# First attention of a two-layer kernel: attention sums in float32r parts over normed tokens, low parts on GpSimd, value weights applied to the sums

## The reference, cut to what matters

```
h = layernorm(x) * (1 + ca) + sa             # per batch; x1 = layernorm(x) before scale and shift
Q = (h @ Wq.T)  K = (h @ Wk.T)  V = (h @ Wv.T)   # per head
attn = softmax(Q @ K.T)                      # 1024 x 1024 per batch and head
out = sum over heads of attn @ V
x = x + ga * out
```

## Time and profile before

| | |
|---|---|
| median of three runs | 3593.37 us (3593.08 to 3593.81) |
| the profiled execution | 3593.08 us, its span 3591.3 us |
| first scores of the attention | 81.67 us into the span |
| last attention output added to x | about 2005 us |
| PE busy | 3069.3 us (85%) |
| DVE busy | 2606.2 us (73%) |
| ACT busy | 1313.8 us (37%) |
| POOL busy | 184.3 us (5%) |

### The profile page before, as it was taken

The page is one execution under the profiler, slowest core; times in us unless marked ns, Lnnn a source line. Parts: engine busy times, 40 slices in busy tenths (PEclk is TensorE's granted clock), DMA queues, the critical chain, the costliest instruction groups (busy, mean ns, idle before and its releaser), DMA issues. The chain is left out here.

```text
span 3591.3 us, 82463 instructions
## 1 busy us (share of the span) xinstructions
PE 3069.3 (85%) x32284; PEld 2455.2 (68%) x32284; DVE 2606.2 (73%) x8488; ACT 1313.8 (37%) x2231; POOL 184.3 (5%) x155
## 2 busy tenths in 40 slices
PE   5999999999999999999999568778888887763555
PEld 2888888888888888888888535555656555551222
DVE  4565766756657667566565579999999999946775
ACT  2544454454545545445454122222222222211222
POOL 0000000000000000000000000000000000002220
PEclk9999999999999999999999856766666666666777
DMA  1000000000000000000000110000000000000000
GB/s 64 1 1 7 1 1 7 1 2 7 1 7 1 1 8 1 1 7 1 7 1 1 45 48 0 0 0 0 0 0 0 0 0 0 0 10 7 12 12 18
DMA packets 6415, 25.26 MB, mean 7 GB/s; under 512 B 1360, under 2 KB 1872, under 8 KB 5840
## 3 DMA queue, kind: packets, MB, share of 16 engines
q1 hardware_dynamic: 6224, 22.57, 1.6%
HBM read 14.18 MB, written 8.39 MB: 6 GB/s over the span
## 5 line engine op out<-in xcount | busy, mean ns | idle before, releaser
L605 PEld LDWEIGHTS obank<-v_one,probs 128*128 128x128 f32 x8192 | 1069.2, 190 | 91.1 <-issue 2.6
L605 PE MATMUL obank<-v_one,probs 128*128 128x129 f32 x8192 | 1078.6, 274 | 0.0
L352 ACT ACTIVATE probs<-bank 128x512 f32<-128x512 f32 x1024 | 583.8, 597 | 746.9 <-PE bank L593 450.9
L442 DVE TENSOR_REDUCE maxes<-ring 128x1 f32<-128x512 f32 x1024 | 659.5, 686 | 129.0 <-PE ring L573 105.7
L592 PE MATMUL bank<-q_hh,k_hl 128*128 128x512 f32 x1024 | 505.2, 493 | 1.1 <-issue 0.7
L593 PE MATMUL bank<-q_lm,k_h 65*128 65x512 f32 x1024 | 406.6, 397 | 0.0
L455 DVE RECIPROCAL recip<-obank 128x1 f32<-128x1 f32 x512 | 83.4, 163 | 414.5 <-PE obank L605 401.2
L573 PE MATMUL ring<-k_hl,q_hh 128*128 128x512 f32 x1024 | 338.4, 410 | 10.4 <-DVE k_hl L434 6.0
L1054 PE MATMUL ring<-up,z 128*128 128x128 f32 x1024 | 175.7, 352 | 128.5 <-DVE parts L971 127.1
L965 DVE TENSOR_TENSOR low_hot<-ids,low_iota 128x16384 f16<-128x16384 f16 x32 | 278.1, 8692 | 9.1 <-ACT ids L865 6.0
L1054 PEld LDWEIGHTS ring<-up,z 128*128 128x128 f32 x1024 | 170.5, 265 | 140.2 <-issue 138.7
(11 more groups left out here) (220 smaller groups left out, 3499.2 us busy)
## 6 DMA issues: line engine op xcount, KB each, us to landing
xt<-in_x SPq DMA_DIRECT2D x8, 512.0 KB, 8.3
out_x<-xt SPq DMA_DIRECT2D x8, 512.0 KB, 2.6
x<-out_x SPq DMA_DIRECT2D x1, 4096.0 KB, 12.1
out_x<-x SPq DMA_DIRECT2D x8, 512.0 KB, 2.6
pk_wq<-in_w_q SPq DMA_DIRECT2D x1, 1024.0 KB, 4.9
pk_wqT<-in_w_qT SPq DMA_DIRECT2D x1, 1024.0 KB, 7.1
wmod_sb<-in_wmod SPq DMA_DIRECT2D x2, 384.0 KB
w_qk_sb<-in_w_qk SPq DMA_DIRECT2D x1, 512.0 KB, 4.3
```

The source lines that it names most:

```text
L352: nc.scalar.activation(probs[:, half, i, :], st[s % 4], ACT.Exp).then_inc(st_free[s % 4], 1)
L442: nc.vector.tensor_reduce(maxes[:, i, k:k + 1], ring[bank_of(at)][:], AX.X, ALU.max).then_inc(rows_maxed, 1)
L605: mm = nc.tensor.matmul(obank[j % 2][:, 0:D + 1], probs[:, half, m, cols], v_one[h % 2][:, m, :], start=(m == 0), stop=(m == TB - 1))
```

## The change: what it does

The change moves the value weights behind the attention sum and splits the probabilities.

- **Sums over normed tokens.** Instead of probs times V, PE forms, for each half of 512 queries, the sum over keys of x1 (the normed tokens before scale and shift, 128 numbers) times the probability, transposed: 128 x 512. The last number of x1 is overwritten with 1, so that the last row of the sums is the softmax sum. `product` does it in three float32r matmuls of 512 columns per step: x1_l times high, x1_h times low, x1_h times high, five steps (LAG) behind the scores, all eight steps of a half into one bank `obank[half]`.
- **Two exps per step.** ACT computes each exp twice: in float32 into `probs` (4 buffers) and rounded to float32r into `probs_h` (8 buffers). POOL subtracts one from the other, 128 x 512, into `probs_l` (`low_part`, 16 per head; LOW_DVE is empty, so none on DVE).
- **Output per half.** ACT copies the finished sums to SBUF (`sums_out`); PE `outputs` multiplies them by the head's output weights in 4 float32 matmuls of 129 columns: three go into `obank[half]`, one into a bank of the ring. That is at step 15 for the first half and step 10 of the next head for the second. DVE `gather_output` then takes the reciprocals (one of 1, one of 3 columns) and adds the four tiles.
- **Output weights.** The scale and shift of the norm are folded into a 128 x 128 matrix per batch (`output_turns`, once at the start, six DVE instructions; POOL `turn_of` copies out the batch's). PE `weights_of` multiplies it by Wv of the head (step 13, one float32 matmul of 128 columns) in place of the 8 of `v_of`; ACT copies it.
- **q and k from parts.** `hT` and `w_qk` are split into float32r high and low parts, and `q_and_k` on PE is 6 float32r matmuls of 512 columns. ACT makes two copies per half rather than three; DVE makes the third, a copy of 64 x 1024 from SBUF to SBUF over both halves. DVE's `q_and_k` moves from the end of a head to step 1 of the next.
- **Row scores** move to steps 3, 4, 5, 7, 8, 9, 11, 12; the row maximum turn to step 14.
- **Tokens.** `first_norm` keeps x1 in `x1_next`; POOL copies and splits it in 8 tiles per batch (`values_of`) around the change of batch. DVE makes the low part of the transposed tokens (`fine_h`, head 6).
- The ring order has, per head, two `"o"` uses and one `"w"` use; an `"o"` is released when all four tiles of its half have been added.

```diff
-STEPS_LOOP = 79
+STEPS_LOOP = 47
+LAG, DEEP = 5, 8
+ROW_STEPS = (3, 4, 5, 7, 8, 9, 11, 12)
+OUT_1, WEIGHTS, MAXIMA, OUT_0 = 10, 13, 14, 15
+LOW_LAG = 2
+LOW_DVE = ()
@@ released
+            if kind == "w":
+                return w_ready, shift(b, n + 1, H)
+            if kind == "o":
+                return o_read, shift(b, 8 * n + 4 * uses[at][2] + 4, 8 * H)
@@ POOL
+            def values_of(b, i):
+                nc.gpsimd.sem_inc(turns, 1)
+                nc.gpsimd.tensor_copy(x1_h[:, i, :], x1_next[:, i, :]).then_inc(x1_h_ready, 1)
+                pool.wait_ge(x1_h_ready, TB * b + i + 1)
+                nc.gpsimd.tensor_tensor(x1_l[:, i, :], x1_next[:, i, :], x1_h[:, i, :].bitcast(F32), ALU.subtract).then_inc(x1_l_ready, 1)
+            def low_part(g, s):
+                i = s % DEEP
+                pool.wait_ge(st_free[s % 4], 4 * g + s // 4 + 2)
+                nc.gpsimd.sem_inc(turns, 1)
+                nc.gpsimd.tensor_tensor(probs_l[:, i, :], probs[:, s % 4, :], probs_h[:, i, :].bitcast(F32), ALU.subtract).then_inc(low_pool, 1)
@@ ACT
-                    nc.scalar.activation(q_hh[s][R:P, cols], bank[0:R, :], ACT.Copy).then_inc(hi_ready, 1)
+            def output_weights(b, h):
+                if not (isinstance(b, int) and b * H + h < 2):
+                    wait_full(b, located(b, "o", h - 2, 1))
+                at = located(b, "w", h)
+                wait_full(b, at)
+                nc.scalar.activation(w_out[h % 2][:, 0:D], ring[bank_of(at)][:, 0:D], ACT.Copy).then_inc(w_ready, 1)
+            def sums_out(b, h, half):
                 g = b * H + h
+                if not (isinstance(g, int) and g == 0):
+                    wait_full(b, located(b, "o", h - 1, half))
+                act.wait_ge(product_done, 2 * TB * g + TB * half + TB)
+                nc.scalar.activation(sums[half][:], obank[half][:], ACT.Copy).then_inc(sum_read, 1)
             def exponentials(b, h, s):
-                act.wait_ge(st_full[s % 4], 4 * g + s // 4 + 1)
-                nc.scalar.activation(probs[:, half, i, :], st[s % 4], ACT.Exp).then_inc(st_free[s % 4], 1)
+                g, i = b * H + h, s % DEEP
+                if s % 2 == 0 and not (isinstance(g, int) and g == 0 and s < DEEP):
+                    act.wait_ge(product_done, 2 * TB * g + s - DEEP + 2)
+                if not (isinstance(g, int) and g == 0 and s < 4):
+                    behind, at = step_before(s, 4)
+                    act.wait_ge(*low_done(g - behind, at))
+                act.wait_ge(st_full[s % 4], 4 * g + s // 4 + 1)
+                nc.scalar.activation(probs[:, s % 4, :], st[s % 4], ACT.Exp)
+                nc.scalar.activation(probs_h[:, i, :], st[s % 4], ACT.Exp).then_inc(st_free[s % 4], 1)
@@ DVE
+                nc.vector.tensor_copy(q_hh[s][R:P, :], q_hh[s][0:R, :].bitcast(F32)).then_inc(q2_ready, 1)
+            def gather_output(link, b, h, half):
+                g, at = b * H + h, located(b, "o", h, half)
+                wait_full(b, at)
+                dve.wait_ge(o_full, 2 * g + half + 1)
+                three = obank[half][:, 0:3 * (D + 1)].rearrange("p (j d) -> p j d", j=3)
+                one = ring[bank_of(at)]
+                t0 = 4 * half
+                nc.vector.reciprocal(recip[:, t0 + 3:t0 + 4], one[:, D:D + 1]).then_inc(steps, 1)
+                link.n += 1
+                link(nc.vector.reciprocal(recip[:, t0:t0 + 3], three[:, :, D]))
+                if h % H != 0:
+                    dve.wait_ge(o_read, 8 * (g - 1) + 4 * half + 5)
+                for j in (3, 0, 1, 2):
+                    t, o = t0 + j, (one[:, 0:D] if j == 3 else three[:, j, 0:D])
+                    ...
+                        nc.vector.scalar_tensor_tensor(acc[:, t, :], o, recip[:, t:t + 1], acc[:, t, :], ALU.mult, ALU.add).then_inc(o_read, 1)
@@ PE
+                    nc.tensor.matmul(bank[:], w_qk_l[:, h % H, :], hT_h[:, cols], start=True, stop=False)
+                    nc.tensor.matmul(bank[:], w_qk_h[:, h % H, :], hT_l[:, cols], start=False, stop=False)
+                    give(at, nc.tensor.matmul(bank[:], w_qk_h[:, h % H, :], hT_h[:, cols], start=False, stop=True))
+            def product(b, h, s):
+                g, half, i = b * H + h, s // TB, s % TB
+                pe.wait_ge(*low_done(g, s))
+                ...
+                high, low = probs_h[:, s % DEEP, :], probs_l[:, s % DEEP, :]
+                nc.tensor.matmul(obank[half][:], x1_l[:, i, :], high, start=(i == 0), stop=False)
+                nc.tensor.matmul(obank[half][:], x1_h[:, i, :], low, start=False, stop=False)
+                nc.tensor.matmul(obank[half][:], x1_h[:, i, :], high, start=False, stop=(i == TB - 1)).then_inc(product_done, 1)
+            def outputs(b, h, half):
+                g = b * H + h
+                at = located(b, "o", h, half)
+                bank = take(b, at)
+                pe.wait_ge(sum_read, 2 * g + half + 1)
+                pe.wait_ge(w_ready, g + 2)
+                for j in (3, 0, 1, 2):
+                    out = bank[:, 0:D + 1] if j == 3 else obank[half][:, j * (D + 1):(j + 1) * (D + 1)]
+                    mm = nc.tensor.matmul(out, sums[half][:, j * P:(j + 1) * P], w_out[h % 2][:], start=True, stop=True)
+                    if j == 3:
+                        give(at, mm)
+                mm.then_inc(o_full, 1)
@@ PE body, per step s
                         scores(b, h, s)
-                        if 3 <= s <= 10 and more:
-                            score_rows(b, h + 1, s - 3)
+                        if s in ROW_STEPS and more:
+                            score_rows(b, h + 1, ROW_STEPS.index(s))
+                        behind, at = step_before(s, LAG)
                         if not (first and h < behind):
-                            products(b * H + h - behind, h - behind, half, i)
+                            product(b, h - behind, at)
+                        if s == OUT_1 and not (first and h == 0):
+                            outputs(b, h - 1, 1)
+                        if s == WEIGHTS and more:
+                            weights_of(b, h + 1)
+                        if s == WEIGHTS and h == H - 2 and not last:
+                            turn_h(b, 1)
+                        if s == MAXIMA and more:
+                            turn_max(b, h + 1)
+                        if s == OUT_0:
+                            outputs(b, h, 0)
```

More of the change, by code:

```diff
@@ L295, in body @@
                     for s in range(2 * TB):
+                        behind, at = step_before(s, LOW_LAG)
+                        if not on_dve(at) and not (first and h < behind):
+                            low_part(g - behind, at)
                         if s == 4 and not (last and h == H - 1):
                             second_k(g + 1, h + 1)
+                        if s == 5 and h == H - 1 and not last:
+                            at_w = located(b, "w", h)
+                            pool.wait_ge(ring_full[bank_of(at_w)], filled(b, at_w))
+                            turn_of(b + 1)
+                        behind, at = step_before(s, LAG)
+                        if at >= TB and ((h == H - 1 and not behind and not last) or (h == 0 and behind and not first)):
+                            now = b if behind else b + 1
+                            if at == TB:
+                                pool.wait_ge(x1_made, now + 1)
+                            pool.wait_ge(product_done, (now * H - 1) * 2 * TB + at + 1)
+                            values_of(now, at - TB)
                         if not first and h == 2 and s == 1:
@@ L304, in _ @@
             second_k(0, 0)
+            pool.wait_ge(turns_made, 1)
+            turn_of(0)
+            pool.wait_ge(x1_made, 1)
+            for i in range(TB):
+                values_of(0, i)
             batches(pool, body)
+            for s in range(LOW_LAG):
+                at = step_before(s, LOW_LAG)[1]
+                if not on_dve(at):
+                    low_part(B * H - 1, at)
             rstd(2 * B)
@@ L419, in first_norm @@
             def first_norm(link, n, b, count):
[L420 removed]
+                norm_step(link, n, tiles_of(b), h_tok[:], row(1, b), row(0, b), count, h_ready, keep=True)
             def second_norm(link, n, b, count):
@@ L504, in _ @@
                 first_norm(link, n, 0, 1)
+            fine_h(0, 0)
             q_and_k(0, 0)
@@ L631, in _ @@
                 score_rows(0, 0, i)
-            v_of(0, 0)
+            weights_of(0, 0)
             turn_max(0, 0)
@@ L635, in _ @@
             batches(pe, body)
-            for i in (6, 7):
-                products(B * H - 1, H - 1, 0, i)
-            for i in range(TB):
-                products(B * H - 1, H - 1, 1, i)
+            for s in range(LAG):
+                product(B - 1, H - 1, step_before(s, LAG)[1])
+            outputs(B - 1, H - 1, 1)
 def build_product_key_table(nc, a, hc, ones, half_neg, ident, banks, wide, w_eff, sim_bias, mean_col,
```

249 lines of the change are left out of this document (147 added, 102 removed).

## The result

| | kernel before | changed kernel |
|---|---|---|
| median of the runs | 3593.22 us (3592.66 to 3593.81) | 3663.78 us (3660.99 to 3664.56) |
| span of the profiled execution | 3591.3 us | 3662.5 us |
| first row maximum | 75.9 us | 83.6 us |
| last row maximum | 1962.4 us | 2038.45 us |
| granted clock of that execution | 1.00 in each window of 300 us from 100 to 1850 | 0.99, 0.97, 0.97, 0.97, 0.96, 0.98 |

The changed kernel is slower: ratio 1.0195, 95% interval [1.0177, 1.0213] (whether by more or less than 2% the interval leaves open). I forecast 3588 with a range up to 3650. The spans differ by 71.2 us: 7.7 before the first row maximum, 68.3 between first and last, -4.8 behind the last. The loss lies in the attention's loop.

What follows compares the result with a forecast made beforehand. PE was taken to bound the attention. Stream -3.2, ring +2.2, q copy +0.35: -0.65 a head, 64 heads -42; heads 1 and 3 +24, head 6 +7, start and end +6: 3588 us; own range 3565 to 3610, wider 3525 to 3650.

Steps and rivals of the forecast that it cites:

- PE's stream: PE's own work per head: 17.8 us removed, 14.6 added, so 3.2 us less.
- Term 1: PE waits for a ring bank behind the outputs until DVE's four additions end: 1.1 us twice a head, 2.2.
- Term 2: Row scores of step 3 wait for DVE's q copy, held by POOL's subtraction: PE stands 0.45, booked +0.35 a head.
- The walk: Step-by-step timing of the engines' queues; for the q copy, its end 3.1 us after ACT's last copies.
- Term 3: Norms in steps 11 to 15 delay the gather of step 15 in heads 1 and 3: 1.7 x 14 = 24 us.
- Head 0: Head 0 with its residual: DVE early enough or no later than now, POOL's lateness within the slack; nothing booked.
- Start and end: Work before the first norm and the first head +5 us, copied sums and outputs behind the last product +1.
- head 6: Second transposition waits for ACT's copy of weights, turned maxima for DVE's low part: 1.0 x 7 = 7 us.
- B: Rival: DVE and POOL take turns everywhere, delaying q copy and norms; 3659 us full price, 3623 half; chance 0.17.
- A: Rival: ports don't matter, the q copy costs 0.1 and heads 1 and 3 nothing; 3548 us; chance 0.20.
- C: Rival: ACT becomes late, so outputs at step 15 wait 0.35 us for the negated maximum; 3610 us; chance 0.10.
- D: Rival: POOL bounds through longer subtractions; at 2.0 us each a head is 33 us, 3820 in all; chance 0.03.

Runs made afterwards that it cites:

- Experiment 1: Changed kernel with the ring bank of the outputs released after the first of four additions: 3594.07 us, ratio 1.0003 to the kernel before.
- Experiment 2: Changed kernel with the third q copy moved from DVE back to ACT: 3614.07 us, ratio 1.0063 to the kernel before.
- experiment 5: Changed kernel with DVE's residual in head 0 moved from step 11 to step 13: 3624.75 us, ratio 1.0091 to the kernel before.
- experiment 4: Changed kernel with the batch loop written out on four engines: 3629.22 us; the same edit of the kernel before: 3585.92 us.
- experiment 3: Changed kernel without POOL's 16 subtractions per head, the second matmul of a product reading the high part: 3560.08 us, ratio 0.9912.
- experiment 7: Kernel with all four mends, norm instructions of heads 1 to 4 spread to steps 6 and 13 to 15 (also called kernel 7): 3720.39 us.
- experiments 7 to 9: Norms spread to step 6 and 13 to 15: 3720.39 us; that with two low parts cut to 8 columns: 3486.27; instead with POOL waiting for DVE: 3493.08.
- all four mends: Changed kernel with early ring release, third q copy on ACT, batch loop written out and residual at step 13 together: 3511.44 us, ratio 0.9779.

## Why the prediction was wrong

- **PE's stream: right.** A plain step starts every 1.165 us and a step with row scores every 1.64 (1.17 and 1.65 forecast); the stream without waits is 26.3 us a head, 3.4 under a plain head of before, for -3.2 forecast.
- **Term 1, the ring waits: right in place, near in size.** Over the stream without waits, 1.4 in front of the second `q_and_k` group and 1.1 around step 11, for 1.1 each. Experiment 1 shows the cause.
- **Term 2, the q copy: mis-sized.** The walk itself was right: it had the copy end 3.1 us after ACT's last copies, behind one subtraction, and the median is 3.13 (the copy takes 1.77 us for 0.68, in 58 of 64 heads over 1.0). But PE's next matmul starts 0.24 us behind the copy's end, for which the walk had nothing, and PE stood 0.7 to 0.8 rather than 0.45, of which 0.35 was booked as the difference to before; step 3 takes some 2.55 us for the 1.64 of an undisturbed one. Experiment 2 puts the copy at 0.9 a plain head and 50 us in all. That plus 0.3 in term 1 turns the forecast gain of 0.65 a head into a loss of 0.1: 0.75 x 64, 48 us of the miss of 76.
- **Term 3, the norms: right in place, near in size.** Booked 1.7 in heads 1 and 3, none in 2 and 4. By PE's steps, step 15 of heads 1 and 3 takes 5.76 and 5.80 us, that of heads 2, 4 and 5 takes 4.86. Then the granted clock fell: in 11 of the 12 heads 2 and 4 of batches 1 to 6, steps 0 and 1 ran at a mean granted clock of 0.56 to 0.62 and took 3.6 to 3.9 us together, 1.2 to 1.6 more than in head 5, of which 0.9 came back, as the q copy was ready for step 3. Counted over whole heads the two norms cost 1.3 and 1.4 us, 2.7 a batch for the 3.4 booked. (The clock had no place in the walk.) The first table shows 0.7 to 0.8 in each of intervals 1 to 4, but that is its mark.
- **Head 0, booked at nothing: the failed step.** "In heads 2 and 4, and head 0 with its residual, the walk finds DVE early enough or no later than now" and "`values_of` ... makes it late by about 1 us, within the slack". POOL's lateness was within PE's slack, but it turned its low parts into one run of 15.7 us. The residual, at its side, took 3.02 and 2.04 us for 1.22 each in the rows of experiment 5, and the last row reductions and with them the output weights queued behind it: PE's step 13 took 4.69 us for 1.30. With POOL idle it takes 2.10, so 2.6 of the 3.4 us are POOL's; the residual's place alone is the rest. Experiment 5 returns 39 us.
- **The jump of the batch loop: not in the prediction at all.** It cost 0.19 us in the trace of before and I took that for its price; in the changed kernel it was 3 us and a clock of 1.2 GHz behind it, some 28 us by the estimate of experiment 4.
- **Start and end:** +7.7 for +5, and -4.8 for +1.
- **The sum of the misses:** plain heads 48; head 0 with the jump, 6.8 in intervals 0 and 1 less 0.8 for the norm and 0.2 for two plain heads, 5.8 a batch, about 38 over six and a half changes of batch; norms -5 and head 6 (0.7 a batch for 1.0) -2; start and end -3: 76, beside 3663.8 - 3588 = 76. The agreement is closer than such estimates are. The residual and the jump give more back singly (39 and 35) than they added, because the kernel before pays at that place too (33.73 against 29.70).
- **The rivals.** B named the right resource and its place, and its full price, 3659, lies beside the measured time, but by its sum, not by its parts: the jump and head 0 were not in it. A is refuted by experiment 3 (POOL idle: -104), C and D by the waits: PE waited neither for a negated maximum nor, beyond 0.9 us, for POOL.

I priced the port as taking turns, one POOL instruction for one of DVE, from two pairs in the earlier trace rows in which POOL had only one instruction to give. For the q copy that held. It did not hold beside a long run: there one or two further subtractions passed in front of the residual in five of seven batches, and four or five in front of the moved norms of experiment 7. The Trainium skill, "SBUF — State Buffer", section "SBUF: two separate sides", says that the lock is held for the whole instruction; experiments 7 to 9 show more: DVE can be kept out for several of POOL's instructions that follow each other without a gap.

## What to carry to other kernels

When an engine takes over work that keeps a second one's port, ask not how long one instruction is but how long the unbroken runs are, and where in them the other engine's instructions fall; a queue that is late but within its slack is one long run, and the other engine may be kept out for all of it. A wait of 1.3 us on purpose, in the right place, was worth 227 us in the same schedule. And when a change makes a saturated engine wait, a loop's jump and the granted clock can cost what they did not before: look them up in the new trace, not in the old one. Last, measure a head by a mark on the engine that bounds: a mark on a late engine moves time between neighbours.

## Not expected of the hardware

- A DVE instruction that met a run of POOL's subtractions in kernel 7 ended 0.03 us (a TENSOR_SCALAR of 8 elements a partition) to 1.1 us (a TENSOR_TENSOR of 1024) behind POOL's run, after 5.65 and 7.94 us; in the changed kernel others were let in earlier. POOL was hardly slowed by it: 1.29 us a subtraction in the median, 1.36 in the mean, 2.28 at most (changed kernel).
- PE's jump at the end of a loop body: 0.19 us in the row shown of the kernel before, whose PE was busy up to it, 2.84 to 3.42 us in the changed kernel, whose PE had just waited, with the granted clock at 0.50 for 5.3 us afterwards. Written out, neither appears at that place.
- The clock elsewhere: with the loop written out PE was busy 272 of 300 us in a window, with stands of 0.7 to 1.4 us three times a head, and the windows' clock held at 0.98 to 1.00. In the changed kernel, behind the late step 15 of heads 1 and 3 (5.7 to 6.1 us), it fell to 0.50; with all four mends it did not fall there.
